# Loading two groups of image 0 and the weights on ScalarE's DMA queue in a fused norm and quantised convolution

## The reference

```
x: (32, 512, 28, 28) f32          # 32 images, 512 channels, 784 pixels
v  = group_norm(x, 32 groups of 16 channels, eps 1e-5)
xg = v in 4 conv groups of 128 channels, rotated by one: perm = [1, 2, 3, 0]
xa = round(clip((xg - lA) / (uA - lA), 0, 1) * 15) / 15
wq = (round(clip((weight - lW) / (uW - lW), 0, 1) * 15) / 15 - 0.5) * 2
y  = per conv group: wq[g] (128x128) times xa[g]      # a 1x1 convolution
y  = relu(batch_norm(y; gamma, beta, running_mean, running_var))
out = x + y + v
```

## Time and profile before

| | |
|---|---|
| median of 3 runs | 259.03 us |
| the profiled execution | 258.41 us |
| its span | 256.7 us |
| TensorE busy | 193.9 us (76%) |
| VectorE busy | 230.0 us (90%) |
| ScalarE busy | 215.2 us (84%) |
| GpSimd busy | 212.0 us (83%) |
| DMA | 103.25 MB, mean 402 GB/s |
| packets of q1 | 18624, 54.86 MB |
| packets of q10 | 15874, 48.18 MB |

### The profile page before, as it was taken

How to read it: one execution, slowest core, us unless ns; L and a number is a source line. 1 busy time by engine, 2 the same in 40 slices (tenths; PEclk the granted TensorE clock), 3 DMA queues, 4 the chain that set the end, 5 groups by cost and what they waited for, 6 DMA issues and landing times.

```text
span 256.7 us, 3463 instructions
## 1 busy us (share of the span) xinstructions
PE 193.9 (76%) x999; PEld 109.3 (43%) x999; DVE 230.0 (90%) x363; ACT 215.2 (84%) x394; POOL 212.0 (83%) x340
## 2 busy tenths in 40 slices
PE   1142996969889888979797997877696969889920
PEld 0132644435454444445443554343444435454510
DVE  2898698999999999999999899999999999969940
ACT  4437898999999999989999889999899888999300
POOL 6126869999999999999999999999999999999100
PEclk9999999797979798988979599999979797979995
DMA  6999999999999999999999999999999999999994
GB/s 225 398 411 411 408 409 406 418 416 417 418 414 418 417 416 418 411 418 416 416 415 416 418 416 413 419 417 415 417 413 418 416 418 409 402 400 402 393 399 193
DMA packets 34516, 103.25 MB, mean 402 GB/s; under 512 B 1202, under 2 KB 1730, under 8 KB 34498
## 3 DMA queue, kind: packets, MB, share of 16 engines
q1 hardware_dynamic: 18624, 54.86, 53.8%
q10 hardware_dynamic: 15874, 48.18, 47.0%
HBM read 51.65 MB, written 51.38 MB: 401 GB/s over the span
## 4 chain that ended last, share of the span: by engine, by line
POOL 52%; DVE 16%; issue 11%; PE 9%; ACT 5%; DMA 2%; DVEq 0%; SPq 0%; POOLq 0%; ACTq 0%
POOL images L413 27%; POOL levels L424 8%; DVE images L482 7%; PE prod L604 6%; DVE stats L460 4%; POOL dev L375 3%; DVE codes L475 3%; PE var_ps L584 3%; POOL dev L378 2%; DMA images<-in_x 2%; POOL scaled L404 2%; ACT levels L270 2%; POOL coef L406 2%; POOL norm L402 1%; ACT unused L242 1%
## 5 line engine op out<-in xcount | busy, mean ns | idle before, releaser
L604 PE MATMUL prod<-codes,w_t 128*128 128x392 bf16 x768 | 160.8, 369 | 7.9 <-DVE codes L475 2.9
L482 DVE SCALAR_TENSOR_TENSOR images<-prod,floor,images 128x784 f32<-128x784 f32 x128 | 128.0, 1019 | 8.5 <-PE prod L604 8.2
L413 POOL TENSOR_SCALAR images<-images,coef 128x784 f32<-128x784 f32 x120 | 123.7, 1042 | 0.0
L604 PEld LDWEIGHTS prod<-codes,w_t 128*128 128x128 bf16 x768 | 79.1, 110 | 81.6 <-issue 24.6
L270 ACT ACTIVATE levels<-images,coef 128x784 int16<-128x784 f32 x95 | 91.3, 1028 | 1.1 <-issue 1.1
L460 DVE BATCH_NORM_STATS2 stats<-images 128x6 f32<-128x392 f32 x136 | 68.9, 551 | 5.4 <-DMA images<-in_x 5.4
L236 ACT ACTIVATE unused<-images 128x784 bf16<-128x784 f32 x60 | 50.7, 847 | 7.5 <-DMA images<-in_x 5.2
L242 ACT ACTIVATE unused<-images,sums 128x784 bf16<-128x784 f32 x60 | 56.1, 939 | 0.1
L475 DVE TENSOR_SCALAR codes<-levels 128x3136 bf16<-128x3136 int16 x32 | 34.7, 1085 | 1.0 <-ACT levels L270 0.7
L584 PE MATMUL var_ps<-dev,avg 128*128 128x8 f32 x128 | 19.6, 280 | 20.0 <-POOL dev L382 20.0
L424 POOL TENSOR_SCALAR levels<-images,coef 128x784 int16<-128x784 f32 x33 | 33.6, 1020 | 0.1
(11 more groups left out here) (66 smaller groups left out, 83.2 us busy)
## 6 DMA issues: line engine op xcount, KB each, us to landing
images<-in_x SPq DMA_DIRECT2D x30, 1568.0 KB, 14.5
out<-images ACTq DMA_DIRECT2D x30, 1568.0 KB, 18.8
images<-in_x SPq DMA_DIRECT2D x8, 392.0 KB, 6.6
out<-images SPq DMA_DIRECT2D x1, 1568.0 KB, 8.8
out<-images SPq DMA_DIRECT2D x4, 392.0 KB, 7.4
w_raw<-in_weight SPq DMA_DIRECT2D x1, 256.0 KB, 6.5
rows<-in_channel_params ACTq DMA_DIRECT2D x1, 8.0 KB, 2.3
limit_row<-in_limits ACTq DMA_DIRECT2D x1, 0.0 KB
```

The source lines that it names most:

```text
L413: nc.gpsimd.tensor_scalar(here, here, coef[:, u % 2, 0, 1, G * j + o:G * j + o + 1], coef[:, u % 2, 1, 1, G * j + o:G * j + o + 1], ALU.mu ...
L482: nc.vector.scalar_tensor_tensor(out=two, in0=prod[:, k % SETS, :, 0:HALF], scalar=floor[:, o:o + 1], in1=two, op0=ALU.max, op1=ALU.add).t ...
L604: done = nc.tensor.matmul(prod[:, k % SETS, h, 0:HALF], w_t[:, part, output_group(g)], codes[:, n % 2, g, h * HALF:(h + 1) * HALF], start= ...
```

## The change

Groups 1 and 2 of image 0 and the weights are issued by ScalarE. SP issues groups 0 and 3 of image 0 and goes on to image 1.

```diff
         @block.sync
         def _(sync):
             for n in range(SINGLE):
-                for g in (0, G - 1, 1, 2):
+                for g in (0, G - 1) if n == 0 else (0, G - 1, 1, 2):
                     sync.dma_start(images[:, n, g], x_v[n][:, g]).then_inc(first_loaded[n][g], DMA)
-                if n == 0:
-                    sync.dma_start(w_raw[:], weight.rearrange("(g o) i -> o g i", o=P)).then_inc(weights_in, DMA)
...
         @block.scalar
         def _(act):
+            act.dma_start(images[:, 0, 1], x_v[0][:, 1]).then_inc(first_loaded[0][1], DMA)
             act.dma_start(rows[:], channel_params.rearrange("k (g p) -> (k g) p", p=P)).then_inc(rows_in, DMA)
             act.dma_start(limit_row[:], limits).then_inc(limits_in, DMA)
+            act.dma_start(images[:, 0, 2], x_v[0][:, 2]).then_inc(first_loaded[0][2], DMA)
+            act.dma_start(w_raw[:], weight.rearrange("(g o) i -> o g i", o=P)).then_inc(weights_in, DMA)
             act.wait_ge(eps_done, 1)
```

## The result

The changed kernel takes 261.7 us (median of 6 runs, 260.31 to 263.8), the one before 258.86 (6 runs, 258.37 to 259.74): ratio 1.0107, 95% interval 1.0083 to 1.0131. It is slower by 2.8 us, beyond the predicted range, which ended at 261.4. The profiled execution took 260.31, the shortest of the six, so the trace shows less than the median: a span of 258.6 us against 256.7.

A forecast was written before the change was run, and what follows sets the result against it. Computation and transfers were taken to end nearly together. Late weights +3.3, regained -0.3, absorbed by slack -2.2 gave +0.8 us on the profiled 258.41, so 259.2, or 259.8 us for the median; range 258.2 to 261.4.

The forecast's parts named there:

- I take 12.6: At the start: the weights on ScalarE's queue land at 12.6 us, between a lower bound of 11.5 and an upper of 13.1.
- one-to-one sharing by packets: DMA engines: two full queues send equal packet counts, taken from 403 of SP's against 400 of ScalarE's at 44 to 50 us.
- count of 785 packets: ScalarE's queue up to the weights' end: 256 of groups 1 and 2, 17 of parameters, 512 of weights; SP sends 785 meanwhile.
- VectorE ready at 9.4 to 9.5: Start of VectorE: ready for the weights at 9.4 to 9.5 us against 9.31, costing 0.1 to 0.2 if they were there.
- 3.3 us later: Start of the computation: delayed 3.3 us (2.2 to 3.8) by VectorE's wait for the weights, 12.6 against 9.3.
- I take the difference of 0.3 us back: Around 208 us: later stores find a shorter queue, so ScalarE's wait to issue shrinks; 0.3 us regained (0 to 1.05).
- Slack there: 2.2 us: Last stores: the slowest DMA engine's backlog absorbs 2.2 us of the 3.0 us slip, leaving 0.8.
- average one of 1.1 us: Last stores: average DMA backlog 2.0 us, less 0.9 from issue to first packets, gives 1.1 us of slack.
- rival 2: Stores of images 29 to 31: slack is only the average 1.1 us, 1.9 us pass through, 260.9 us median; chance 0.20.
- rival 1: Weights' transfer: small packets go in bursts past much of image 1, landing at 10.7; time unchanged, 259.0 median; chance 0.22.
- Rival 3: Transfers from 2 to 8 us: two queues fill the start, weights not late, end 1.2 us earlier, 257.8; chance 0.08.
- The signs that I had named: Trace times expected if the forecast held: weights, image 1's statistics, first coefficients, last store's issue; last landings 2 to 3 us shorter.

## Why the prediction was wrong

The sign of each term and the mechanism held: the weights on ScalarE's queue are late, VectorE waits for them with image 1's statistics behind the wait, and the transfers run dry at the end. The sum of +0.8 us against a measured +2.8 failed by sizes, of three terms.

- **"I take 12.6"** for the landing of the weights. It was 2.67 + 10.7 = 13.4 us, beyond my upper bound of 13.1 (14.1 in the second profile of the changed kernel). The one-to-one sharing by packets is right for this stretch, as the queues from 9 to 10 us show:

```profile
q1 hardware_dynamic: 124, 0.34, 84.6%
q10 hardware_dynamic: 126, 0.06, 21.3%
```

The count of 785 packets on each side supposed that ScalarE's queue has something to send all the time. From 5 to 6 us it had not:

```profile
q1 hardware_dynamic: 147, 0.41, 103.2%
q10 hardware_dynamic: 6, 0.00, 1.1%
```

Group 2 was issued at 2.27 us and its packets came only after 6. In that microsecond SP's queue moved 0.4 MB of what lies behind, which at 409 GB/s is 1 us that the weights lost. In the version with the large packets ScalarE's queue sent 7 packets in the same microsecond, and they landed late too. The count of 785 was also short. The queues' totals show 16 packets more for each large DMA than it has rows of data (SP's 18624 before are 31 x 528 + 12 x 144 + 528), and ScalarE's queue had 34 for the parameters and limits, not 17. That makes 850 up to the end of the weights, beside 864 of SP's up to the end of image 1: by equal counts still nearly the same moment. The only time from issue to first packet that the prediction has is 0.9 us, of the last store; the first store of the kernel before, issued at 40.18 us, had nothing in ScalarE's queue until after 43.5, and I did not use it.

- **VectorE ready at 9.4 to 9.5**: 9.90, since the third group landed at 8.86. This cost nothing, as the weights were later.

- **"3.3 us later"**: 4.1, by the two above.

- **"I take the difference of 0.3 us back"**: nothing came back, the slip had grown to 4.4 at image 30's store. The idle time of ScalarE before 212.49 is not there in the changed kernel, and the time is longer all the same: it was not on the path.

- **"Slack there: 2.2 us"**: I chose the lagging DMA engine's backlog over the average one of 1.1 us, because the span ends with the slowest. The delays of 4.1 and 5.0 us show 1.2 and 1.5, others 1.1 to 2.3. The average backlog was the nearer measure in all but one of them; rival 2, priced with 1.1 us of slack and given 0.20, was the better model. Of the 2.0 us between +0.8 and +2.8, 0.8 are the landing, 0.3 the gain that did not come, and 0.9 are left for the slack. With the slack of the two delays in its place the sum is 4.1 - 0 - 1.5 to 4.1 - 0 - 1.2, so +2.6 to +2.9. The profiled execution alone would not have shown the error: with 260.31 against 258.41 us and a slip of 4.1 it gives 2.2.

By rival 1, bursts, the weights would have landed at 10.7. For the changed kernel the 124 packets beside 126, and the landing at 13.4, refute it: there the small ones did not pass the large ones in fewer turns. The page "DMA: Bandwidth & Descriptors" of the Trainium skill, section "Queues, rings and completion order", says that an engine drains a packet of some 9 to 17 descriptors before it turns to the other queue. What the profile counts as a packet is smaller, one run of 512 or 3136 bytes (0.06 MB in 126 of them). My rival drew the wrong conclusion from it: turns of equal length on both queues give equal counts, whatever the length, and the sum is that of the forecast. The changed kernel doesn't tell turns of one from turns of eight, since a DMA engine moved only some eight of each in that microsecond. The version with only the weights moved has the burst, 250 packets beside 16 in half a microsecond. Why the weights got it there and not in the changed kernel is open, and so is how far one-to-one sharing can be counted on.

Rival 3, the fuller start, came true as far as the transfers go: 409 GB/s from 4 to 8 us (387 in the second profile). With a late computation it was worth nothing; the version that has it without late weights gained 0.24%, though that the one comes from the other is argued and not shown. I had held against it that the DMA engines were busy in that stretch. They were, and the same share of busy time moved more bytes. The section "Issuing engines are not separate DMA queues" of the same page of the Trainium skill says that a second issuing engine saves only sequencer time. The runs neither confirm nor refute it for this stretch: with two queues it had 409, 388 and 280 GB/s, against 323 with one, so a second queue as such doesn't fill it, but some arrangements with two are fuller than the one with one.

The signs that I had named: the weights at 12.6 (13.42), image 1 at 15.3 (16.17), the first coefficients at 26 (26.77), the last store's issue at 250 (251.6), and shorter landings at the end (6.4 us instead of 7.4 to 8.8).

## What to carry to other kernels

A transfer of many small packets should not stand on a queue beside one that is full of large packets if somebody waits for it: count the packets ahead on both queues, not the bytes, allow for the time until its queue begins to send, and look at the trace, since one arrangement here didn't follow the count. Before a wait is moved or its transfer re-queued, read what stands behind it in program order; image 1's statistics did not need the weights, and moving them ahead removed nearly all of the loss. Where the computation and the transfers end together, measure the slack with a plain delay (spare instructions, transfers untouched): it gives the exchange rate between lateness and time. Take several lengths: here the delays of 4.1 and 5.0 us cost 3.0 and 3.5 us, while one of 3.5 cost 1.2 in one measurement and 2.3 in another.

## What the runs showed of the hardware

- From issue to first packet it took 0.9 us for the first of SP's last stores, but more than 3 us for later issues of ScalarE's queue, while SP's queue was busy: group 2, issued at 2.27, had packets after 6 us, the weights in the version with only them, issued at 1.79, after 5 us, and the first store, issued at 40.18, after 43.5. What holds them back was not tried.
- The stretch from 4 to 8 us has a rate of its own: 323 GB/s before, 409 in the changed kernel, 388 with the weights on SP's queue, 280 with the parameters first. It also varies from one execution to the next: 387 in the second profile of the changed kernel, and 298 to 336 in the delayed versions of the kernel before, whose DMAs at the start are the same. The order of the issues changes it by more than that, and the DMA engines count as nearly fully busy in the first three (share 1.00, 1.03, 1.04) and not in the last (0.87). The dip of the changed kernel looks alike: from 60 to 62 us it has 260 GB/s at a share of 0.98, with loads alone in the queues. Why is open.
- Two full queues shared the DMA engines one to one by packets (403 to 400 of equal size, 124 to 126 with small ones on one side), but in one version 250 small packets went beside 16 large ones in half a microsecond.
- A transfer's last packets can come long after most of it: with only the weights moved, 446 packets of ScalarE's queue, nearly all of them the weights', went from 5 to 7 us, and the last landed at 11.9.
